# The last expert stage: gate and up biases folded into the weights, instead of a bias product per block

## The reference

```python
out = jnp.zeros_like(xs)
for e in range(E):
    h = jax.nn.silu(xs @ Wg[e] + bg[e]) * (xs @ W1[e] + b1[e])
    out = out + we[:, e:e + 1] * (h @ W2[e] + b2[e])
```

## Time and profile before

| | us |
|---|---|
| median of 3 runs | 1203.97 |
| lowest, highest | 1200.14, 1209.07 |
| the profiled execution, its own time | 1207.58 |
| its span, first to last instruction | 1205.8 |
| its layer 3 stage: first instruction | 956.8 |
| its block loop: first product of a block (a transpose) | 1074.6 |
| its last gate-and-up product | 1174.4 |

### The profile page before, as it was taken

The page is one execution under the profiler, slowest core; times in us unless marked ns, Lnnn a source line. Parts: engine busy times, 40 slices in busy tenths (PEclk is TensorE's granted clock), DMA queues, the critical chain, the costliest instruction groups (busy, mean ns, idle before and its releaser), DMA issues. The chain is left out here.

```text
span 1205.8 us, 24315 instructions
## 1 busy us (share of the span) xinstructions
PE 965.2 (80%) x8100; PEld 760.1 (63%) x8115; DVE 722.3 (60%) x1962; ACT 572.4 (47%) x1195; POOL 459.0 (38%) x518
## 2 busy tenths in 40 slices
PE   6799885769992888888789999999997656339991
PEld 5566664769992655555666667766676545229990
DVE  4678645546665677773567666676445657535554
ACT  2577751335552367765354554455432543225552
POOL 1256563533444221211351334343433514733332
PEclk8899995879995899999799999999997976559995
DMA  8121110111212022111400101111114500111113
GB/s 278 48 65 49 56 44 12 37 43 42 58 42 70 18 61 68 55 56 39 137 18 2 26 14 37 37 37 38 37 37 131 194 1 11 35 44 46 52 46 105
DMA packets 80904, 67.05 MB, mean 56 GB/s; under 512 B 6753, under 2 KB 73592, under 8 KB 80402
## 3 DMA queue, kind: packets, MB, share of 16 engines
q1 hardware_dynamic: 76274, 57.04, 16.4%
q0 software_dynamic: 4512, 8.47, 2.2%
HBM read 39.30 MB, written 26.58 MB: 55 GB/s over the span
## 5 line engine op out<-in xcount | busy, mean ns | idle before, releaser
L444 DVE TENSOR_REDUCE a_rowmax<-a_banks 128x4 f32<-128x1024 f32 (+1 forms) x112 | 136.7, 1221 | 64.9 <-PE a_banks L689 30.6
L2252 POOL TENSOR_TENSOR a_both<-a_probs 128x512 f32<-128x512 f32 x64 | 86.4, 1350 | 159.7 <-ACT a_probs L2477 159.7
L549 ACT ACTIVATE a_probs<-a_banks 128x1024 f32<-128x1024 f32 x112 | 114.9, 1026 | 59.9 <-PE a_banks L675 48.4
L1149 POOL DMA_INDIRECT acc<-m_result,m_yb x77 | 75.4, 980 | 140.7 <-DVE m_result L1440 74.2
L2477 ACT ACTIVATE a_probs<-a_banks 128x1024 f32<-128x1024 f32 x64 | 65.5, 1024 | 88.6 <-PE a_banks L2536 88.6
L1549 ACT ACTIVATE m_gate<-m_banks 128x352 f32<-128x352 f32 (+1 forms) x93 | 42.8, 460 | 95.3 <-PE m_banks L1739 92.9
L2383 DVE TENSOR_REDUCE a_rowmax<-a_banks 128x4 f32<-128x1024 f32 x64 | 78.0, 1219 | 14.9 <-PE a_banks L2513 14.9
L1142 POOL DMA_INDIRECT rows<-m_yrow,m_idx x64 | 63.4, 991 | 51.1 <-issue 21.8
L2550 PE MATMUL a_banks<-a_probs,a_V 128*64 128x256 f32 x512 | 69.4, 392 | 0.6 <-ACT a_craw L2466 0.6
L717 PE MATMUL a_banks<-a_probs,a_V 128*32 128x256 f32 x768 | 61.6, 393 | 8.3 <-ACT a_raw L542 6.9
L1420 DVE TENSOR_TENSOR m_h<-m_banks,m_gate 128x342 f32<-128x342 f32 (+1 forms) x55 | 28.4, 517 | 61.5 <-ACT m_gate L1549 55.9
(11 more groups left out here) (369 smaller groups left out, 2856.4 us busy)
## 6 DMA issues: line engine op xcount, KB each, us to landing
rows<-fill SPq DMA_DIRECT2D x16, 520.0 KB, 4.3
a_factor<-recip_rows SPq DMA_DIRECT2D x28, 256.0 KB, 4.6
rows<-fill SPq DMA_DIRECT2D x15, 455.0 KB, 3.9
m_yb<-rows SPq DMA_DIRECT2D x77, 65.0 KB
f_expert<-in_experts SPq DMA_DIRECT2D x16, 257.5 KB, 3.0
m_parts<-acc SPq DMA_DIRECT2D x16, 256.0 KB, 5.0
bias<-in_bias_zero SPq DMA_DIRECT2D x1, 3248.0 KB, 20.9
e_gu_lo<-in_gu SPq DMA_DIRECT2D x1, 2736.0 KB
```

What stands on the lines that cost most here:

```text
L444: nc.vector.reduce_max(o, src, AX).then_inc(rowmax_ready, 1)
L549: nc.scalar.activation(probs[h][:, k, :, :], ps[:, 4:6, :], ACT.Exp, scale=SCALE).then_inc(exp_done, 1)
L1149: nc.gpsimd.indirect_dma_start(acc.rearrange("k n d -> (k n) d"), bass.IndirectOffsetOnAxis(yb[b % YB][:, P:P + 1].bitcast(U32), 0), resul ...
L2252: nc.gpsimd.tensor_tensor(both[u % 4][:, :, :], p[:, :, 0, :], p[:, :, 1, :], ALU.add).then_inc(both_ready, 1)
```

## The change

The rows of a block have mean zero. So one is added to each element of the rows (`y + 1`), and the gate and up weights are replaced by `(I - 1/128) W + b/128` in every row: the ones meet the centred weights in nothing and the bias in b, and the rows meet the bias part in nothing. `centre_weights`, a new part of `split` on PE, makes these weights into PSUM with float32 products, and ACT and DVE take high and low parts from there. The bias products of gate and up go; that of down stays. The splits are placed in later steps, and the zero-filled bias buffer shrinks.

```diff
-BIAS = NE * (2 * F_EXP[3] + P)
+BIAS = NE * P
-    splits = {0: [0, 1, 2], 1: [3], 5: [4, 5], 6: [6, 7]}
+    splits = {4: [0, 1], 5: [2, 3], 6: [4, 5, 6, 7]}
...
+        def both_halves(gu):
+            return gu.rearrange("p (k f) -> p k f", k=2)
+
+        def centred_gu(e):
+            b = 2 * (e % 2)
+            return ps[:, b:b + 2, 0:width]
...
-                sp.dma_start(bias_raw[:, :], bias).then_inc(bias_loaded, 16)
+                sp.dma_start(bias_raw[:, :], dram["bias3"]).then_inc(bias_loaded, 16)
+                sp.dma_start(centre[:, :], dram["centre"]).then_inc(centre_loaded, 16)
+                sp.dma_start(bias_gu[:, :], dram["bias_gu"]).then_inc(centre_loaded, 16)
+                sp.dma_start(bias_row[:, :, :], dram["bias_row"]).then_inc(centre_loaded, 16)
...
-                nc.vector.tensor_tensor(gu_lo, raw_gu, gu_hi.bitcast(F32), ALU.subtract)
+                nc.vector.tensor_tensor(both_halves(gu_lo), centred_gu(e), both_halves(gu_hi).bitcast(F32), ALU.subtract)
...
-                nc.vector.tensor_tensor(y_lo[i % 3][:, :], ps[:, 4, 0:P], y_hi[i % 3][:, :].bitcast(F32),
-                                        ALU.subtract).then_inc(y_lo_ready, 1)
+                if by_distance:
+                    nc.vector.scalar_tensor_tensor(y_lo[i % 3][:, :], ps[:, 4, 0:P], 1.0, y_hi[i % 3][:, :].bitcast(F32),
+                                                   ALU.add, ALU.subtract).then_inc(y_lo_ready, 1)
...
-                nc.scalar.activation(gu_hi, raw_gu, ACT.Copy)
+                act.wait_ge(centred_ps, split_at[e])
+                nc.scalar.activation(both_halves(gu_hi), centred_gu(e), ACT.Copy)
...
-                nc.scalar.activation(y_hi[i % 3][:, :], ps[:, 4, 0:P], ACT.Copy).then_inc(y_hi_ready, 1)
+                if by_distance:
+                    nc.scalar.activation(y_hi[i % 3][:, :], ps[:, 4, 0:P], ACT.Identity, bias=ones_f[:, 0:1]).then_inc(
+                        y_hi_ready, 1)
...
-                    if by_distance:
-                        mm(o, bias_one[:, :], biases[:, e, s], start=False, stop=False)
...
+            def centre_weights(e):
+                if e == 0:
+                    pe.wait_ge(w["loaded"], w["parts"])
+                    pe.wait_ge(centre_loaded, 48)
+                    pe.wait_ge(c_yT_ready, RUNS)
+                    pe.wait_ge(c_v_ready, RUNS)
+                    pe.wait_ge(c_qk_ready, RUNS)
+                if e >= 2:
+                    pe.wait_ge(split_ready, e - 1)
+                raw_gu, _, _ = raw_parts(w, layer, e)
+                for k in range(2):
+                    s, o = slice(k * width, (k + 1) * width), ps[:, 2 * (e % 2) + k, 0:width]
+                    mm(o, centre[:, :], raw_gu[:, s], start=True, stop=False)
+                    last = mm(o, bias_row[:, e, :], bias_gu[:, s], start=False, stop=True)
+                last.then_inc(centred_ps, 1)
...
+                if kind == "split":
+                    centre_weights(r)
```

More of the change, by code:

```diff
@@ L944, in mixed_events, with experts @@
     return events + [("slot", s) for s in range(-2, W + 2)]
-def experts(nc, g, layer, key, w, mix=None, bias=None, out=None):
+def experts(nc, g, layer, key, w, mix=None, dram=None, out=None):
     width = F_EXP[layer]
@@ L1020, in experts @@
             bias_one = st.sb("bias_one", [P, P], F32R)
+            centre = st.sb("centre", [P, P])
+            bias_gu, bias_row = st.sb("bias_gu", [NE, 2 * width]), st.sb("bias_row", [NE, NE, P])
             flat = [p[:, :, :, :].rearrange("p k t d -> p (k t d)") for p in parts]
@@ L1047, in experts @@
         if by_distance:
-            dist_ready, c2_ready, c2_ps, bias_loaded, bias_high, bias_low, bias_placed, stored = (st.sem(n) for n in (
-                "dist_ready", "c2_ready", "c2_ps", "bias_loaded", "bias_high", "bias_low", "bias_placed", "stored"))
+            (dist_ready, c2_ready, c2_ps, bias_loaded, bias_high, bias_low, bias_placed, stored, centre_loaded,
+             centred_ps) = (st.sem(n) for n in (
+                 "dist_ready", "c2_ready", "c2_ps", "bias_loaded", "bias_high", "bias_low", "bias_placed", "stored",
+                 "centre_loaded", "centred_ps"))
             (c_in_var, c_in_rstd, c_y_ready, c_yT_ps, c_yT_ready, c_qk_ps, c_qk_ready, c_v_ps, c_v_ready, c_z_ps,
@@ L1236, in split @@
                 gu_hi, gu_lo, down = weights(e)
-                raw_gu, raw_full, raw_rest = raw_parts(w, layer, e)
-                nc.vector.tensor_tensor(gu_lo, raw_gu, gu_hi.bitcast(F32), ALU.subtract)
+                _, raw_full, raw_rest = raw_parts(w, layer, e)
+                nc.vector.tensor_tensor(both_halves(gu_lo), centred_gu(e), both_halves(gu_hi).bitcast(F32), ALU.subtract)
                 nc.vector.tensor_tensor(down[:, 0:2, 1, :], raw_full, down[:, 0:2, 0, :].bitcast(F32), ALU.subtract)
@@ L1406, in low_y @@
                     dve.wait_ge(gu_ps, i - 2)
-                nc.vector.tensor_tensor(y_lo[i % 3][:, :], ps[:, 4, 0:P], y_hi[i % 3][:, :].bitcast(F32),
-                                        ALU.subtract).then_inc(y_lo_ready, 1)
+                if by_distance:
+                    nc.vector.scalar_tensor_tensor(y_lo[i % 3][:, :], ps[:, 4, 0:P], 1.0, y_hi[i % 3][:, :].bitcast(F32),
+                                                   ALU.add, ALU.subtract).then_inc(y_lo_ready, 1)
+                else:
+                    nc.vector.tensor_tensor(y_lo[i % 3][:, :], ps[:, 4, 0:P], y_hi[i % 3][:, :].bitcast(F32),
+                                            ALU.subtract).then_inc(y_lo_ready, 1)
             def hidden(i):
@@ L1542, in high_y @@
                     act.wait_ge(gu_ps, i - 2)
-                nc.scalar.activation(y_hi[i % 3][:, :], ps[:, 4, 0:P], ACT.Copy).then_inc(y_hi_ready, 1)
+                if by_distance:
+                    nc.scalar.activation(y_hi[i % 3][:, :], ps[:, 4, 0:P], ACT.Identity, bias=ones_f[:, 0:1]).then_inc(
+                        y_hi_ready, 1)
+                else:
+                    nc.scalar.activation(y_hi[i % 3][:, :], ps[:, 4, 0:P], ACT.Copy).then_inc(y_hi_ready, 1)
             def gates(i):
@@ L1765, in down @@
                 if by_distance:
-                    last = mm(o[:, 0:P], bias_one[:, :], biases[:, e, 2 * width:2 * width + P], start=False, stop=True)
+                    last = mm(o[:, 0:P], bias_one[:, :], biases[:, e, :], start=False, stop=True)
                 last.then_inc(down_ps, 1)
+            def centre_weights(e):
[13 more added lines that the diff above has]
+                last.then_inc(centred_ps, 1)
             expert = {}
@@ L2798, in program @@
         selected_ffn(nc, g, 2, "ffn2", a["experts2"], load_next=load_last)
-        experts(nc, g, 3, "moe3", w3, mix="att3", bias=a["bias3"], out=out_dram)
+        experts(nc, g, 3, "moe3", w3, mix="att3", dram=a, out=out_dram)
 def packed(inputs):
@@ L2877, in packed @@
     a["moe3"] = np.hstack([t("L3_ffn_centroid"), iota])
-    a["bias3"] = np.hstack([f32("L3_ffn_bg"), f32("L3_ffn_b1"), f32("L3_ffn_b2")]).reshape(BIAS_ROWS, -1)
+    a["bias3"] = f32("L3_ffn_b2").reshape(BIAS_ROWS, -1)
+    a["bias_gu"] = np.hstack([f32("L3_ffn_bg"), f32("L3_ffn_b1")])
+    a["bias_row"] = np.repeat(np.eye(NE, dtype=np.float32)[:, :, None] / P, P, axis=2)
+    a["centre"] = (np.eye(P) - 1.0 / P).astype(np.float32)
     a["bias_zero"] = np.zeros((P, BIAS), np.float32)
```

## The result

The changed kernel is slower: 1210.99 us in the median of 22 runs against 1203.30 of 22 for the kernel before, a ratio of 1.0063 with an interval of 1.0045 to 1.0082, some 7.6 us. I had forecast 1193.1, with a range of 1186 to 1200.

What follows compares the result with a forecast made beforehand. It took a two-slot ring through DVE and PE's sequencer to bound the block loop, and a chain across engines the part before; 6.3 from the loop plus 4.6 before it made 10.9, giving 1193.1 us, range 1186 to 1200.

Steps and rivals of the forecast that it cites:

- What a centring costs: PE before the loop: 8 float32 passes per expert at 0.30 us each, 2.4 per expert, double at 1.2 GHz.
- pre-loop gain of 4.6: Part before the block loop: first transpose at 1069.9 instead of 1074.55, so 4.6 us won.
- Splits gone from steps 0 and 1: Early steps before the loop: waits behind splits on DVE and ACT vanish, 9.5 us won (7.6 to 10.6).
- The new wait: End of the part before the loop: SP's first load waits for the map chain (4.1 us) behind DVE's last split.
- The loop: Block loop: without the gate and up bias products a slot falls from 2.54 to 2.38 us, 6.3 won in all.
- One added to the rows: Block loop: `high_y` on ACT at most 0.1 us longer, hidden; `low_y` on DVE stays at 0.28.
- Rival (4): Before the loop: centring passes in steps 4 to 6 all at half clock, 0.60 each; 5.6 us slower, 1209.6; chance 0.08.
- turning point: Before the loop: slower once about two thirds of the passes forecast at full clock run at half clock.
- Rivals (1) to (3): PE alone limits the loop, 1186.9, chance 0.13; sends stay last, 1189.2, 0.13; late splits eat the early gain, 1197.7, 0.21.
- (3): Last step before the loop: late splits end the map 4.5 us later, only the loop gains, 1197.7; chance 0.21.

Runs made afterwards that it cites:

- e5: The changed kernel with the bias operands of the centring padded with zeros from 8 to 128 rows; ratio 0.9911 to the kernel before.
- e1: The changed kernel run and profiled again with nothing edited; ratio 1.0061 to the kernel before.
- e10: The changed kernel with the centring product also cut to 8 rows, leaving out most of the gate and up weights; ratio 1.0009 to the kernel before.
- e3: The kernel before without the gate and up bias products of the block loop, nothing else changed; ratio 0.9936 to the kernel before.
- e2: The kernel before with only the splits moved to after steps 4, 5 and 6, no centring, bias products kept; ratio 0.9899 to the kernel before.
- e9: The changed kernel with bias operands padded to 128 rows and the block map put before the last four experts' splits; ratio 0.9863 to the kernel before.

## Why the prediction was wrong

**What failed: "What a centring costs".** I scaled a float32 pass by its columns, from products of 128 rows, to 0.30, and had PE come back to full clock after 2 us of dense work in step 5 and 3.5 in step 6. Half of the centring passes have 8 rows, and I priced them by columns alone. The runs showed 0.38 a pass at full clock and 0.72 at half, and no return of full clock at all in steps 5 and 6. By my own groups:

| experts | forecast | changed kernel | with 128 rows (e5) |
|---|---|---|---|
| 0 and 1, step 4 | 4.8 | 6.1 | 4.9 |
| 2 and 3, step 5 | 5.7 | 11.6 | 6.9 |
| 4 to 7, step 6 | 11.5 | 23.0 | 11.9 |

The forecast and the changed kernel differ by 18.7. My pre-loop gain of 4.6, less 18.7, is a loss of 14.1; the measured loss is 14.0. The intermediate times agree: in e1, moved back by the 2.9, PE's router in step 5 ends 1.3 after my time, the passes of step 5 7.1, the ranks of run 3 7.1, the last pass 18.6 and the first transpose 18.7. Each us of the centrings went straight through to the loop's start, so this one term holds all of the error.

By the terms of my sum it divides so. I had some 55 of the 64 passes at full clock (2 and 3.5 us cold, at 0.60 a pass, are 9 passes); 16 were. The other 39 at 0.30 more each are 11.7. The longer pass (0.38 for 0.30 in 16 of them, 0.72 for 0.60 in 48) is the other 7.0.

The experiments tell the cause. Shown by e5 and e10: a change between shapes of 8 and 128 rows adds 0.10 a pass at full clock (0.38 against 0.29) and 0.15 at half (0.72 against 0.57), and with 8-row passes, alone or in turn with full ones, the clock didn't return. How much each part is worth, if the turns are taken away first and the few rows second, follows from e10, of one shape but cold: in steps 5 and 6 its groups are 2.3 and 4.5 shorter than the changed kernel's (the change of shape) and 2.4 and 6.6 longer than e5's (the clock). With the 1.2 of step 4, where the changed kernel was at full clock, that is 8.0 for the turns and 9.0 for the clock, of the 17.0. Taken away the other way round the clock's share would be larger, since a pass with turns costs 0.34 more at half clock and one without them 0.28; no run shows that order.

Why a change of shape costs this is not shown. The rows of the weight loads in the last step of e1 have the two loads of a product close together and then 0.94 with none, while in e5, also at half clock, a load comes with each pass and 0.23 lies between; that would fit a load that can't run ahead across the change, but nothing here tests it. Nor do the runs tell at how many rows the clock returns; I tried 8 and 128 only. The kernel before has one hint against carrying this to every narrow product: in its first attention, products of 24 and 25 rows, some side by side, stand among others in a dense stretch at full clock.

```profile
60.00:65.00 5.00, 4.85 (x57) 3.45 (x58) 4.79 (x7) 3.69 (x8) 2.69 (x4) 1.00 0.32 100
```

```profile
64.86 0.28 PE L675 MATMUL a_banks<-a_QT,a_KT 25*128 25x256 f32 x2
```

That 120 of the 128 rows hold zeros, in every other product of e5, didn't keep the clock from returning.

**What held, with its numbers.** *Splits gone from steps 0 and 1*: 9.5 forecast. The router of run 2 ended 73.5 after the stage's first product before, and 64.0 after: 9.5. The scores of run 0 were on DVE 13.0 after it instead of 17.4, so 4.4 of it came there (4.9 forecast). *The new wait*: the map chain behind the last split as the last link, ahead of SP's first load: the chain of waits has it so, the map takes 4.1, and the first transpose is 2.8 to 2.9 behind it. *The loop*: 6.3 forecast, 6.3 measured; slots of 2.38 forecast, 2.385 measured (it was 2.54), with 1.49 from the end of a result to the next slot's first gate product (before: 1.55), and PE idle there for 0.27 - 0.11 = 0.15 a slot (0.15 forecast). e3 has the same from the loop's edit alone. *One added to the rows*: `high_y` went from 272 ns to 362, hidden; `low_y` stayed at 0.28. With passes near my price the rest of the sum stood: in e5 the three groups take 23.7 (forecast 22.0), pre-loop is 3.8 less than before (forecast 4.6), the stage 10.2 less (forecast 10.9). That e5's span (1194.0) and its ratio on the median of before (1193.3) meet the forecast's 1194.9 and 1193.1 still closer is in part luck, since its stage also began 1.6 earlier, in work that the change doesn't touch.

**The rivals.** Rival (4) had the right mechanism in its main part: centring cold, from the third expert on. I gave it 0.08, with 5.6 us slower; 7.6 was measured. That the two are so close is in part luck: it had all 64 passes at 0.60, where 16 took 0.38 and 48 took 0.72. I had put its turning point at two thirds of the passes that I had at full clock, and 39 of those 55 were cold; by its own price that alone would have cost 11.7, 0.8 more than the 10.9 to be won. The rest of the loss is the longer pass, which none of the rivals had. What misled me was the sentence against it, "in all dense stretches the clock came back". The dense stretches that I had read, in the mixed part and at the loop's start, are of products with 128 rows; none has 8, so the sentence had no row for the case. The Trainium skill was in the same place: "TensorE: Matmul & The Clock Gate", Part 1 ("What's actually happening") says that activity releases the throttle; this trace doesn't agree with it as it stands, since PE was busy for 23.00 of 23.00 us, half of the passes with 8 rows, and the granted clock stayed at 0.50. The same page, under "Why this matters for your kernels", has one product of 32 rows take as long as one of 128; e10 agrees for 8 rows (0.57 a pass at half clock, as with 128 rows in e5), which is why columns alone looked like a fair price. Rivals (1) to (3) all fall: PE was not the loop's limit (e3), the sends were last in e2, and as it seems in e9, where the centring was gone or the map moved, and (3) had the right place, the last step, but 4.5 us for it.

## What to carry to other kernels

A float32 product with 8 rows cost as much here as a full one, and more where it stood between full ones; stretches of them held PE at half clock for 18.5 and 23 us, with PE busy throughout. Padding a small operand with zeros to 128 rows turned a loss of 0.6% into a gain of 0.9%, with not one pass less. But the order of the work, moved with the same edit, brought as much by itself (e2): measure such a side change alone before crediting the main one. And when an engine is given new work in a stretch where its clock is low, look for a dense stretch of the same shape in the trace before assuming that the clock will return; if there is none, work out the sum at the cold price too and give it a real chance.

## What was not expected of the hardware

- PE busy for 23.0 us without a pause at 0.50 (8 and 128 rows in turn), and for 18.5 us (8 rows only). With 128 rows, zeros in 120 of them in every other product, full clock came back 4.5 us into the centrings of step 5 of e5.
- The clock fell from full to half in the middle of a dense row of 8-row passes (e10, step 4, at about 1024.4, some 1.6 us after the first of them).
- A float32 pass of 342 columns: 0.29 at full clock and 0.57 at half if its neighbours have as many rows, 0.38 and 0.72 if 8 and 128 rows take turns.
- Moving the read of the next block's expert two steps forward in PE's queue made the loop slower by 0.06 a slot.
